# The start of a fused AdaLN and mixture kernel: q made by streaming W3 over cond, three of its chunks turned between the first products, one weight chunk rounded on VectorE

## The reference, cut to what matters

```python
# B, N, D = 64, 64, 512; cond is 64 x 256; E = 6 experts of rank R = 16, the best 2 are kept
q      = relu(cond @ W3 + b3)                        # 64 x 512, one row per batch
x1     = (N * x + sum(x over N)) * q[:, None, :]
y      = relu(x1 @ W2 + b2)
base   = y @ W_base + b_base
shared = (y @ A_s) @ B_s
gates  = softmax(y @ W_router + b_router)
routed = sum over the top 2 experts e of gates_e * (y @ A_r[e]) @ B_r[e]
out    = x + base + shared + routed
```

## Time and profile before

| | us |
|---|---|
| median of 3 runs | 230.59 (230.21 to 230.68) |
| the profiled execution | 230.53 |
| its span, first to last instruction | 228.8 |
| PE busy | 224.0 (98% of the span) |
| DVE, ACT, POOL busy | 176.1, 110.2, 107.0 |
| first matmul of the first product starts | 12.53 |
| first matmul of the down projection starts | 23.83 |
| last matmul's results handed to DVE | 223.6 |

### The profile page before, as it was taken

How to read it: one execution, slowest core, us unless ns; L and a number is a source line. 1 busy time by engine, 2 the same in 40 slices (tenths; PEclk the granted TensorE clock), 3 DMA queues, 4 the chain that set the end, 5 groups by cost and what they waited for, 6 DMA issues and landing times.

```text
span 228.8 us, 2915 instructions
## 1 busy us (share of the span) xinstructions
PE 224.0 (98%) x982; PEld 183.1 (80%) x982; DVE 176.1 (77%) x323; ACT 110.2 (48%) x230; POOL 107.0 (47%) x99
## 2 busy tenths in 40 slices
PE   7999999999999999999999999999999999999994
PEld 3987888888888888888888888888888788888883
DVE  0595979899979979699758899999996969382334
ACT  3178631545426345779326496344676375331010
POOL 4079444058125865889887201349988700000000
PEclk9999999999999999999999999999999999999999
DMA  6999902704049495004429844111213742002044
GB/s 194 324 240 230 276 27 53 165 3 185 10 122 261 181 229 171 15 0 182 181 39 222 150 181 141 48 19 17 82 47 127 287 148 84 0 15 47 27 165 183
DMA packets 32917, 29.05 MB, mean 127 GB/s; under 512 B 5841, under 2 KB 23317, under 8 KB 32902
## 3 DMA queue, kind: packets, MB, share of 16 engines
q1 hardware_dynamic: 31090, 28.69, 44.0%
q10 hardware_dynamic: 1812, 0.17, 0.6%
HBM read 18.89 MB, written 8.39 MB: 119 GB/s over the span
## 4 chain that ended last, share of the span: by engine, by line
PE 94%; DMA 2%; DVE 1%; ACT 1%; SPq 1%; issue 0%; DVEq 0%
PE m_ps L1354 77%; PE hT L1354 11%; PE m_ps L1390 5%; DMA x_nat<-in_x_dram 2%; DVE x_nat L1037 1%; PE m_ps L1382 1%; SPq L394 1%; PE m_ps L1331 0%; PE m_ps L1344 0%; ACT qT L676 0%; ACT W_hi L682 0%; ACT x_hi L687 0%; PE hT L1344 0%; DVEq L1036 0%
## 5 line engine op out<-in xcount | busy, mean ns | idle before, releaser
L487 POOL TENSOR_TENSOR xs<-xs,qT 128x512 f32<-128x512 f32 x22 | 24.1, 1096 | 46.7 <-DVE xs L911 30.8
L1354 PE MATMUL m_ps<-Wb_lo,y_hi 128*128 128x512 f32 x116 | 45.1, 389 | 0.0
L1354 PE MATMUL m_ps<-Wb_hi,y_hi 128*128 128x512 f32 x116 | 45.1, 389 | 0.0
L1354 PE MATMUL m_ps<-Wb_hi,y_lo 128*128 128x512 f32 x116 | 45.1, 389 | 0.0
L659 ACT ACTIVATE y_hi<-m_ps,condT 128x512 fp32r<-128x512 f32 x30 | 20.7, 692 | 17.5 <-PE m_ps L1354 10.0
L1354 PEld LDWEIGHTS m_ps<-Wb_hi,y_hi 128*128 128x128 f32 x116 | 21.8, 188 | 4.5
L1354 PEld LDWEIGHTS m_ps<-Wb_hi,y_lo 128*128 128x128 f32 x116 | 21.8, 188 | 4.5
L1354 PEld LDWEIGHTS m_ps<-Wb_lo,y_hi 128*128 128x128 f32 x116 | 21.8, 188 | 4.5
L926 DVE TENSOR_TENSOR y_lo<-m_ps,y_hi 128x512 fp32r<-128x512 f32 x30 | 20.2, 678 | 5.4 <-ACT m_ps L660 5.4
L1354 PE MATMUL m_ps<-x_hi,W_hi 128*128 128x512 f32 x61 | 23.7, 389 | 0.0
L1354 PE MATMUL m_ps<-x_hi,W_lo 128*128 128x512 f32 x61 | 23.7, 389 | 0.0
(11 more groups left out here) (189 smaller groups left out, 494.4 us busy)
## 6 DMA issues: line engine op xcount, KB each, us to landing
out_dram<-x_nat SPq DMA_DIRECT2D x32, 256.0 KB, 2.5
x_quart<-in_x_dram SPq DMA_DIRECT2D x28, 256.0 KB, 4.8
x_nat<-in_x_dram SPq DMA_DIRECT2D x7, 1024.0 KB, 5.5
gatesT<-wT SPq DMA_DIRECT2D x24, 48.0 KB
x_nat<-in_x_dram SPq DMA_DIRECT2D x4, 256.0 KB, 4.0
W_f<-in_L_cond_W_dram SPq DMA_DIRECT2D x4, 256.0 KB, 6.2
Wb_f<-in_L_ffn_W_base_dram SPq DMA_DIRECT2D x1, 1024.0 KB, 8.8
W_sb<-in_L_cond_W_dram SPq DMA_DIRECT2D x2, 256.0 KB, 5.4
```

Of the source, the lines that this page charges most:

```text
L487: return nc.gpsimd.tensor_tensor(per_batch(tile), per_batch(tile), qT[:, c, BG * g:BG * (g + 1)].unsqueeze(2).to_broadcast([P, BG, N]), AL ...
L1354: mm = nc.tensor.matmul(psum, lhsT, rhs, start=start and i == 0, stop=stop and i == len(terms) - 1)
```

## The change

The diff, with the declarations of semaphores left out:

```diff
-    WARM_LOAD, WARM_W3, WARM_HALF, WARM_Q = 8, 1, 2, 1
+    WARM_LOAD, WARM_W3, WARM_Q = 8, 1, 1
...
-        q_ps = m1_ps
+        x_third = xs[0][:, KC - 1, :]
+        HEAD_ORDER = (0, 1, 3, 2)
+
+        q_rows_ps, q_turned_ps = m2_ps[2], m1_ps[2]
+        q_rows = xs[1][0:B, 0, :]
...
-            for c in range(KC):
+            for c in HEAD_ORDER:
                 sp.dma_start(W2_f[:, c, :], W2.rearrange("(p c) n -> p c n", c=KC)[:, c, :]).then_inc(W2_loaded[c], 16)
...
-            for c in range(KC):
-                pool.wait_ge(W2_hi_ready, c + 1)
+            for n, c in enumerate(HEAD_ORDER):
+                if n == 3:
+                    pool.wait_ge(qT_ready, KC)
+                    pool.wait_ge(x1_sum_ready, 3)
+                    scaled(x_third, 0, KC - 1).then_inc(x_third_ready, 1)
+                if n == 0:
+                    pool.wait_ge(W2_first_ready, 1)
+                else:
+                    pool.wait_ge(W2_hi_ready, n)
                 W_rest(W2_lo[:, c, :], W2_f[:, c, :], W2_hi[:, c, :], W2_lo_ready)
...
             def q_relu(c):
 
-                act.wait_ge(q_done, c + 1)
-                nc.scalar.activation(qT[:, c, :], q_ps[c][:, 0:B], ACT.Relu,
+                act.wait_ge(q_done, 1 if c == 0 else KC)
+                q_ps = m1_ps[0][:, 0:B] if c == 0 else q_turned_ps[:, (c - 1) * B:c * B]
+                nc.scalar.activation(qT[:, c, :], q_ps, ACT.Relu,
...
             q_relu(0)
+            x1_split_head(0)
+            act.wait_ge(q_rows_done, 1)
+            nc.scalar.activation(q_rows, q_rows_ps[0:B, :], ACT.Copy).then_inc(q_rows_copied, 1)
+            W2_split(1)
             q_relu(1)
-            W2_split(0)
             q_relu(2)
-            x1_split_head(0)
             q_relu(3)
+            W2_split(3)
             x1_split_head(1)
-            W2_split(1)
             W2_split(2)
-            x1_split_head(2)
-            W2_split(3)
+            x1_split_head(3)
             act.wait_ge(Wd_loaded, 16 * (2 + KC))
             nc.scalar.activation(Wd_hi[:, :, :], Wd_f[:, :, :], ACT.Copy).then_inc(Wd_hi_ready, 1)
-            x1_split_head(3)
+            x1_split_head(2)
...
             sum_head(0)
+            add_head(0)
             sum_head(1)
             scale_head(0)
+            dve.wait_ge(W2_loaded[0], 16)
+            nc.vector.tensor_copy(W2_hi[:, 0, :], W2_f[:, 0, :]).then_inc(W2_first_ready, 1)
+            add_head(1)
+            rest_head(0)
             scale_head(1)
-            rest_head(0)
+            sum_head(3)
+            add_head(3)
+            rest_head(1)
             sum_head(2)
+            add_head(2)
             scale_head(2)
-            rest_head(1)
-            sum_head(3)
-            scale_head(3)
+            rest_head(3)
             rest_head(2)
-            rest_head(3)
...
             y_rest_single(0, 1)
-            total(1, 0)
+            sum_x(1, 0)
             y_rest_single(0, 2)
+            y_rest_single(0, 3)
+            add_sum(1, 0)
             turn_x(1, 1)
-            y_rest_single(0, 3)
             total(1, 1)
...
+            def q_stream(k):
+
+                mm = nc.tensor.matmul(q_rows_ps[0:B, :], condT[:, cond_cols(k)], W3_sb[:, k, :], start=k == 0, stop=k == QC - 1)
+                if k == QC - 1:
+                    mm.then_inc(q_rows_done, 1)
+
+            def q_turn(c):
+
+                nc.tensor.transpose(q_turned_ps[:, (c - 1) * B:c * B], q_rows.rearrange("b (f c) -> b c f", c=KC)[:, c],
+                                    ident[0:B, 0:B]).then_inc(q_done, 1)
...
                 pe.wait_ge(x1_hi_ready, 1)
-                pe.wait_ge(W2_hi_ready, 1)
-                for m in range(KC - 1):
-                    pe.wait_ge(qT_ready, m + 1)
-                    chunk(m, 0, W2_hi, x_hi)
+                pe.wait_ge(W2_first_ready, 1)
+                pe.wait_ge(qT_ready, 1)
+                chunk(0, 0, W2_hi, x_hi)
+                chunk(1, 0, W2_hi, x_hi)
+                pe.wait_ge(q_rows_copied, 1)
+                chunk(KC - 1, 0, W2_hi, x_hi)
+                for c in range(1, KC):
+                    q_turn(c)
                 pe.wait_ge(W2_lo_ready, 1)
-                for m in range(KC - 1):
+                for m in (0, 1, KC - 1):
                     chunk(m, 0, W2_lo, x_hi)
                 pe.wait_ge(qT_ready, KC)
-                chunk(KC - 1, 0, W2_hi, x_hi)
-                chunk(KC - 1, 0, W2_lo, x_hi)
+                chunk(2, 0, W2_hi, x_hi)
+                chunk(2, 0, W2_lo, x_hi)
...
                 for tiles in ((0, 1), (2, 3)):
-                    for k in range(KC // 2, KC):
+                    for n, k in enumerate(HEAD_ORDER[KC // 2:], KC // 2):
...
             pe.wait_ge(condT_copied, 1)
+            pe.wait_ge(W3_loaded[0], 16)
+            q(0, 0)
+            keep_warm(WARM_Q)
+            pe.wait_ge(W3_loaded[1], 16)
+            q(1, 0)
             for k in range(QC):
-                pe.wait_ge(W3_loaded[k], 16)
-                for c in range(KC - 1):
-                    q(k, c)
-                keep_warm(WARM_HALF if k == 0 else WARM_Q)
-            for k in range(QC):
-                q(k, KC - 1)
+                q_stream(k)
```

More of the change, by code:

```diff
@@ L684, in x1_split_head @@
             def x1_split_head(c):
-                act.wait_ge(x1_full_ready, c + 1)
-                nc.scalar.activation(x_hi[:, c, :], head_ps[c][:, :], ACT.Copy).then_inc(x1_hi_ready, 1)
+                if c == KC - 1:
+                    act.wait_ge(x_third_ready, 1)
+                else:
+                    act.wait_ge(x1_full_ready, c + 1)
+                nc.scalar.activation(x_hi[:, c, :], x_third if c == KC - 1 else head_ps[c][:, :],
+                                     ACT.Copy).then_inc(x1_hi_ready, 1)
             q_relu(0)
+            x1_split_head(0)
+            act.wait_ge(q_rows_done, 1)
+            nc.scalar.activation(q_rows, q_rows_ps[0:B, :], ACT.Copy).then_inc(q_rows_copied, 1)
+            W2_split(1)
             q_relu(1)
-            W2_split(0)
             q_relu(2)
-            x1_split_head(0)
             q_relu(3)
+            W2_split(3)
             x1_split_head(1)
-            W2_split(1)
             W2_split(2)
-            x1_split_head(2)
-            W2_split(3)
+            x1_split_head(3)
             act.wait_ge(Wd_loaded, 16 * (2 + KC))
             nc.scalar.activation(Wd_hi[:, :, :], Wd_f[:, :, :], ACT.Copy).then_inc(Wd_hi_ready, 1)
-            x1_split_head(3)
+            x1_split_head(2)
             act.wait_ge(Wb_loaded, 16)
@@ L933, in sum_head, with add_head @@
                                         ALU.add).then_inc(vsum_head_ready, 1)
-                dve.wait_ge(vsum_head_ready, c + 1)
+            def add_head(c):
+                dve.wait_ge(vsum_head_ready, HEAD_ORDER.index(c) + 1)
                 nc.vector.scalar_tensor_tensor(
-                    out=per_batch(head_ps[c][:, :]), in0=per_batch(head_ps[c][:, :]), scalar=float(N),
+                    out=per_batch(x_third if c == KC - 1 else head_ps[c][:, :]), in0=per_batch(head_ps[c][:, :]), scalar=float(N),
                     in1=vsum_head[:, c, :].unsqueeze(2).to_broadcast([P, BG, N]),
@@ L948, in rest_head @@
             def rest_head(c):
-                dve.wait_ge(x1_hi_ready, c + 1)
-                nc.vector.tensor_tensor(x_lo[:, c, :], head_ps[c][:, :],
+                dve.wait_ge(x1_hi_ready, HEAD_ORDER.index(c) + 1)
+                nc.vector.tensor_tensor(x_lo[:, c, :], x_third if c == KC - 1 else head_ps[c][:, :],
                                         x_hi[:, c, :].bitcast(F32), ALU.subtract).then_inc(x1_lo_ready, 1)
             sum_head(0)
+            add_head(0)
             sum_head(1)
             scale_head(0)
+            dve.wait_ge(W2_loaded[0], 16)
+            nc.vector.tensor_copy(W2_hi[:, 0, :], W2_f[:, 0, :]).then_inc(W2_first_ready, 1)
+            add_head(1)
+            rest_head(0)
             scale_head(1)
-            rest_head(0)
+            sum_head(3)
+            add_head(3)
+            rest_head(1)
             sum_head(2)
+            add_head(2)
             scale_head(2)
-            rest_head(1)
-            sum_head(3)
-            scale_head(3)
+            rest_head(3)
             rest_head(2)
-            rest_head(3)
             dve.wait_ge(const_ready, 3)
@@ L1378, in m1 @@
                 mm.then_inc(m1_done, 1)
+            def q_stream(k):
[5 more added lines that the diff above has]
+                                    ident[0:B, 0:B]).then_inc(q_done, 1)
             def q(k, c):
-                mm = nc.tensor.matmul(q_ps[c][:, 0:B], W3_sb[:, k, :].rearrange("p (f c) -> p c f", c=KC)[:, c],
+                mm = nc.tensor.matmul(m1_ps[0][:, 0:B], W3_sb[:, k, :].rearrange("p (f c) -> p c f", c=KC)[:, c],
                                       condT[:, cond_cols(k)], start=(k == 0), stop=(k == QC - 1))
@@ L1425, in m1_first @@
                             chunk(m, k, W2_lo, x_hi)
```

(4 more changed lines are left out.)

15 lines of the change are left out of this document (8 added, 7 removed).

## The result

| | before | changed |
|---|---|---|
| median of the time, 6 runs each | 230.29 (230.21 to 230.68) | 232.07 (231.65 to 233.49) |
| ratio, 95% interval | | 1.0086 (1.0065 to 1.0107) |
| the profiled execution: time, span | 230.53, 228.8 | 233.49, 230.8 |
| first product starts | 12.53 | 11.54 |
| first product's third part resumes | 18.71 | 20.04 |

The changed kernel is slower by 1.8 us, and the interval of the ratio makes that 1.5 to 2.5. Forecast were 231.3 and slower by 0.75. The sign is right, but the change measured is more than twice that size, and 232.07 lies outside the range given, whose end was 231.8.

What follows compares the result with a forecast made beforehand. The prediction took DVE's delivery of x_lo to PE as what bounds the first product's end. PE's resumption at 19.46 against 18.71 added 0.75 to the profiled 230.53, giving 231.3, range 230.2 to 231.8.

Steps and rivals of the forecast that it cites:

- What bounds: First product: its end is set by DVE's delivery of x_lo, not by when PE begins; 1.3 gained at the start is lost.
- the block: First product: POOL's Wd_lo, begun 0.15 ahead, holds DVE's rest_head(3); PE resumes at 19.46 against 18.71, +0.75; chance 0.58.
- R: Start of ACT's relu of q's chunk 1, taken as 12.7 (12.65 to 13.0); DVE's and POOL's later steps count from it.
- Rival A: DVE's rest_head(3) gets SBUF before POOL's Wd_lo; PE goes on at 18.4 to 18.5, time 230.3; chance 0.24.
- the stream: PE makes q's rows in two full-float32 matmuls of 512 columns: four records of 0.41, from about 9.2 to 10.8.
- The copy: ACT copies q's rows after rounding chunk 0, at 11.05 or a little later, for 0.6; q's turns wait for it.
- Everything after 23.83: PE from the down projection on: no holes, so a shift of the first product's resumption at 18.71 reaches the end at full size.
- B: Rival: stream of W3 at 0.60 a record or worse, R 13.4, PE goes on at 20.2, time 232.0; chance 0.08.
- C: Rival: DVE quicker than summed, nothing blocked, PE passes the third matmul at 18.1, time 229.9; chance 0.10.

Runs made afterwards that it cites:

- experiment 3: Changed kernel with q made as in the kernel before (all chunks turned directly, no stream, copy or turns of its rows): 230.57, ratio 1.0011.
- experiment 4: Changed kernel with chunk 3's sum and addition moved into DVE's wait for q's chunk 1, and POOL's multiplication one place earlier: 230.53, ratio 1.0007.
- experiment 1: Changed kernel with POOL's Wd_lo made to wait until DVE's rest of chunk 3 is done: 230.89, ratio 1.0029.
- experiment 5: Changed kernel with one long-met wait more in DVE's list, ahead of rest_head(0): 231.53, ratio 1.0053.
- experiment 6: Kernel before with one entry less in DVE's list, its wait for the constants carried by turn_x(1, 1): 230.82, ratio 1.0015.
- second comparison: Changed kernel run again unaltered, beside new runs of the kernel before: 231.86 against 230.30, ratio 1.0078.
- experiment 2: Changed kernel with chunk 3 left in its bank, DVE multiplying it by q in place of POOL: 231.16, ratio 1.0042.
- experiment 7: experiment 4 with the one wait more of experiment 5, and q's turns ahead of the third product matmul: 229.76, ratio 0.998.
- experiment 8: experiment 4 with the one wait more of experiment 5: 229.71, ratio 0.9976.
- experiment 9: Changed kernel with one entry less in DVE's list, its wait for the constants moved to turn_x(1, 1): 231.74, ratio 1.0076.

## Why the prediction was right in sign and short in size

**What bounds, and the block: right.** The step "So `rest_head(3)` ends at R + 4.86 + 1.29 + 0.55 = R + 6.70, and PE goes on at R + 6.76" was met to a hundredth or two: R + 6.71 and R + 6.76, with the rest at R + 5.00 for R + 5.01 and Wd_lo at R + 4.88 for R + 4.86. The Trainium skill, GPSIMD Engine Reference, section Specifications, speaks of shared, contended access. The runs show its size here: DVE stands until POOL's end, and its pass ends 0.55 behind that, in the changed kernel and in experiments 3 and 4 alike. They show the other direction too: in experiment 3 POOL's pass was lengthened to 1.70 by a DVE rest that had begun first. Rival A was decided by a margin of 0.12, where 0.15 was forecast; experiment 1 gives the price of the block, 1.03.

**R: 0.2 too early.** The relu of chunk 0 came at 9.80 and, in the second profile, at 9.06, on both sides of the 9.44 forecast; that is the landing of x. From it to R the forecast has 12.7 - 9.44 = 3.26, and both profiles have 3.48. The term that was too small is the stream: 0.41 a record was taken, four took 1.93, so 0.48. The copy began 11.60 - 9.80 = 1.80 behind the relu in place of 1.61, which is 0.19 of the 0.22. Counted from a relu of chunk 0 at 9.44, R would be 12.92, inside its range (12.65 to 13.0). That the copy was only 0.19 late is in part luck: the stream was 0.29 longer than taken and began 0.07 later against the relu, but the copy began 0.04 behind its end, where 0.2 was allowed. The Trainium skill, FP8 and Floating Point Precision, section TensorE Precision Notes, came closer than my bounds' middle: by its four passes both matmuls were estimated at 1.8, and 1.9 was measured.

**"Everything after 23.83 follows PE's list without a hole, so a shift of the resumption at 18.71 goes to the end of the program at full size": this step failed.** The shift did go through at full size, but the sentence took the rest of the program for unchanged. So what lies behind the first product was put at nothing. I looked at the order of the second group for late data only, and there it cost nothing, as I said. I didn't look at where the entries of DVE's list come to stand once one is gone from the front. In place of nothing the runs showed 0.41 on DVE and 0.5 on PE there (experiments 5 and 6), the largest part of what the forecast fell short by, and none of my rivals had it. Why number 64 costs that stays open.

**The sum again.** 0.75 forecast, 0.22 for R, 0.4 to 0.5 for the second place: 1.4 to 1.5, and the span's median rose by 1.45 in the second comparison. The time rose by more, 1.78 here and 1.56 in the second comparison. The remainder, 0.1 to 0.3, lies outside the span. Of 84 executions of the changed kernel and of experiments 1, 2, 4, 5, 7, 8 and 9, 29 have more than 1.95 us around the span, up to 3.5; of 23 executions of experiments 3 and 6, and of 75 of the kernel before beside all these, none has more than 1.9. So it goes with the streamed q and its copy and turns, which experiment 3 alone of the changed versions leaves out; that rests on the 11 executions of experiment 3, and no run was made for it. What it is stays open: no profile here shows anything outside its span.

**The other rivals.** B (a stream of 0.60 or worse) gave 232.0, near the time measured, for a wrong reason: R was 0.2 late against the forecast, not 0.7. C (DVE quicker, nothing blocked) fell, although DVE's rounding took 0.42, in the range of 0.3 to 0.7: it runs in the shade of q.

## What to carry to other kernels

When a change lets an engine start earlier by taking longer detours for its inputs, find what ended last before and sum again up to there; the gain of 1 us at the start here was gone by 18 us, because q's other chunks came later, DVE idled 1.25 with work behind the wait in its list, and its last pass was blocked. Two passes over SBUF, one on DVE with both inputs there and one on POOL that reads it too, took turns here rather than overlap, so a few tenths in the order of the two claims decide over a microsecond. And a stretch far behind the edit, in code that it doesn't touch, can change its timing by the mere number of entries ahead of it in an engine's list: compare the intervals there, not only the places that the edit is about.

## What the runs showed of the hardware that I had not expected

- DVE, idle and waiting for PE, started an instruction about 0.41 later when it was number 64 of its list (counted from 0) than when it was number 63, 65 or 66. Twelve profiles agree: 23.11 to 23.13 behind the down projection in the six with number 64, 22.70 to 22.72 in the six others. One entry more or less makes the difference. That a fetch of instructions is behind it was the thought that led to the runs; they show the place and the size, not the cause, and whether later multiples of 64 cost the same where they are exposed was not tried.
- Where a rest on DVE (both inputs in SBUF) and a pass of POOL met, whichever began second was held: DVE 1.71 for 0.68, with POOL 0.12 ahead of it, POOL 1.70 for 1.29, with DVE 0.39 ahead of it. The held DVE pass ended 0.54 to 0.56 behind the end of the POOL pass that it met, in all eight profiles in which this rest was held (both of the changed kernel, experiments 3, 4, 5, 7, 8 and 9). A rest that reads a bank stayed at 0.68 beside POOL (experiment 2 at 16.03, the kernel before at 17.97).
- In full float32 a matmul of 512 columns with 64 columns of weights left two records of 0.48, about 0.95 in all, some four times the 0.23 of float32r at the same granted clock of 1.0. DVE rounds 128x512 from SBUF to float32r in 0.42, against 0.68 to 0.70 for its passes with two inputs.
- The time around the span, 1.7 to 1.9 in all 75 executions of the kernel before beside the experiments, was over 1.95 in a third of those with the streamed q.
